# One DVE operation for the block scales of two tensors, residual additions and a context snapshot at other places of the step: an attention and FP4 FFN block on one core

## Chip, cores and metric

One core of a Trainium2 chip runs the whole program. The metric is the device time of one execution in microseconds (us), a median over runs. Five engines work side by side, each on its own instruction stream, and meet through semaphores: PE (TensorE, matmuls), DVE (VectorE), ACT (ScalarE), POOL (GpSimd) and SP (SyncE, which issues nearly all DMAs).

## What is computed

x has 8 sequences of 2048 tokens with 256 features. Cut to what matters:

```
xn = layernorm(x)
# causal linear attention over buckets of 64 tokens, 16 heads of 16
q, k, v = split(xn @ W_qkv.T);  q = softmax(q, -1) / 4;  k = exp(k)
context, k_sum = exclusive running sums over buckets of k^T v and of k
attn = (q @ context) / max(q . k_sum, 1e-6)
# FFN, every operand of a product quantized in blocks of 16 to FP4 (E2M1)
scale = max(|block|) / 6, at least 1e-12;  v -> grid(v / scale) * scale
h = silu(Q(xn) @ Q(w_gate).T) * (Q(xn) @ Q(w_up).T)
out = x + attn @ W_out.T + Q(h) @ Q(w_down).T
```

## The kernel before, in words

The 16384 tokens are cut into 128 tiles of 128 tokens (the same bucket of 64 tokens of two sequences), and the weights are quantized once at the start. There is no scheduler: each engine has a hand-written function `step(n, d)` that handles tile k = 2n + d, and each engine runs all its steps in that written order. `par` is d, `odd` is 1 - d, and most buffers are double by that parity. The first and last steps are written out, the rest are hardware loops of two steps.

One step works on several tiles at once. In step k:

- **PE** does `project_qkv(k+1)` (q, k, v into two PSUM banks of `unit`), `bucket(k)` (the numerators into `nump`, then the sums into `ctxp`), `gate_up(k, 0)` and `gate_up(k, 1)` (the two halves of the FFN's 704 columns), `transpose_q(k+1)` (L1101, two fp32 transposes into `trp`), `project_att(k-2)` (L1074 to L1078 into `outp`) and `project_h(k-2)` (L1165 to L1168 into `outp`). `project_att(k-2)` waits until DVE has added up tile k-3, since both use `outp`.
- **ACT** does `high_att`, `exp_k`, `exp_q(k+1)` (L556, waits for `shift_q`), the wide copies of the scales (`scales_x` L587, `scales_h` L602), the tanh of both halves (L580), `factor_of_row` (L596), `normalise(k+3)` (L526), `mean_of(k+4)` (L498), `high_xn(k+3)` (L535), `copy_qt(k+1)` (L564, after PE's transposes), `squares_of(k+4)` (L510) and last `snapshot(k+1)` (L617, eight activations that copy the context out of PSUM once PE's `bucket(k)` is done).
- **POOL** does `low_att(k-1)` (L411: att minus its high fp16 part, after ACT's `high_att`), `low_xn(k+3)` (L418, the same for xn after `high_xn`) and `rstd_of(k+4)` (L426 to L436, four operations on one column, after `squares_of`).
- **SP** issues the transposing DMAs `turn_xq(k+1)`, `turn_att(k-1)`, `turn_h(k-1)`, `turn_xn(k+3)` in that order, and every second step a load and a store.
- **DVE** has the longest list: `scale_x(k+1)` (L933, L935), `block_max_x(k+2)` (L834), `block_max_h(k-1)` (L827), `block_scales` (L843 for x, L847 for h), `max_q(k+1)` (L764), `over_one` (L854 row maximum of h's scales, L859 reciprocal of all 60 scales), `row_scale` (L866), `shift_q(k+1)` (L773), `over_row` (L873), the two divisions `over_scales_h` (L880) and `over_scales_x` (L887), the two roundings `round_hx` (L901, L909), between them and behind them the two parts of `add_up(k-3)` (L958, L963), then gate, up, attention and `scale_h(k-1)` (both parts L922).

`block_scales` before is two instructions on neighbouring parts of one tile `blk` (44 columns of h, 16 of x), each multiplying by a constant and taking the maximum with a floor: a constant for x, a value in SBUF (`h_floor`) for h:

```
nc.vector.tensor_scalar(xblk[:, 1, :], xblk[:, 0, :], SIX_TIE * 2.0 ** 11, XS * TINY * 2.0 ** 11, ALU.mult, ALU.max)
nc.vector.tensor_scalar(hblk[:, 1, :], hblk[:, 0, :], SIX_TIE * 2.0 ** 11, h_floor[:, :], ALU.mult, ALU.max)
```

Of the kernel before, what the change touches and what calls it, by code (L numbers as in the profile page):

```python
# [5 lines left out]
def linear_attention_fp4_ffn_block(nc, x, wqkv_t, wout_t, wgate, wup, wdown, out):  # L6
# [59 lines left out]
    with ctx:  # L66
# [75 lines left out]
        hblk, xblk = blk[:, :, 0:FB], blk[:, :, FB:FB + XB]  # L142
        xs_hi = sb("xs_hi", [P, 2 * XB], bf16)
# [65 lines left out]

        hx_step = sem("hx_step")  # L210
# [50 lines left out]
        def _(sp):  # L261
# [31 lines left out]
            def turn_xq(t, par):  # L293
                if not is_tile(t):
                    return
                sp.wait_ge(xq_step, after(t, 6))
                sp.sem_inc(sp_turn, 1)
                if begun(t - 2):
                    sp.wait_ge(gu_done, after(t - 2, 2))
                sp.sem_inc(sp_turn, 1)  # L300
                sp.dma_start_transpose(xqt[:, par, :, :].rearrange("p s (c k) -> p (s c) k", k=P),
                                       xq_s[:, par, :, :].rearrange("p s k -> p (s k)")).then_inc(xqt_done[par], 16)

            def turn_h(t, par):
                if not is_tile(t):
                    return
                sp.wait_ge(hq_step, after(t, 9))
# [156 lines left out]
        def _(act):  # L464
# [49 lines left out]
            def normalise_waits(t):  # L514
                if not is_tile(t):
                    return
                act.wait_ge(rstd_step, after(t, 4))
                if begun(t - 2):
                    act.wait_ge(xn_lo, after(t - 2))
                if begun(t - 2):  # L520
                    act.wait_ge(xq_step, after(t - 2, 6, 3))
# [61 lines left out]
            def scales_x(t):  # L583
                if not is_tile(t):
                    return
                act.wait_ge(xq_step, after(t, 6, 2))
                nc.scalar.activation(xs_hi[:, :].rearrange("p (b i) -> p b i", i=2), twice(xblk[:, 1, :]), ACT.Copy)\  # L587
                    .then_inc(x_scaled, 1)

            def factor_of_row(t, par):  # L590
                if not is_tile(t):
                    return
                act.wait_ge(hq_step, after(t, 9, 4))
# [4 lines left out]
            def scales_h(t):  # L598
                if not is_tile(t):
                    return  # L600
                act.wait_ge(hq_step, after(t, 9, 5))
# [18 lines left out]
            def step(n, d):  # L620
# [6 lines left out]
                tanh_gate(k, 0, par)  # L627
                normalise_waits(k + 3)
# [45 lines left out]
        def _(dve):  # L674
# [139 lines left out]
            def times_up(t, half, par):  # L814
# [3 lines left out]
                if begun(t - 2):  # L818
                    dve.wait_ge(hq_step, after(t - 2, 9, 6))
# [20 lines left out]
            def block_scales(t, u):  # L840
                if is_tile(u):
                    dve.wait_ge(xq_step, after(u, 6, 1))
                    nc.vector.tensor_scalar(xblk[:, 1, :], xblk[:, 0, :], SIX_TIE * 2.0 ** 11, XS * TINY * 2.0 ** 11, ALU.mult, ALU.max)\  # L843
                        .then_inc(xq_step, 1)
                if is_tile(t):
                    dve.wait_ge(hq_step, after(t, 9, 1))
                    nc.vector.tensor_scalar(hblk[:, 1, :], hblk[:, 0, :], SIX_TIE * 2.0 ** 11, h_floor[:, :], ALU.mult, ALU.max)\  # L847
                        .then_inc(hq_step, 1)

            def over_one(t, u):  # L850
                do_h, do_x = is_tile(t), is_tile(u)
# [39 lines left out]
            def round_hx(t, u, part):  # L891
# [4 lines left out]
                if part == 0:  # L896
                    if do_h:
                        dve.wait_ge(hq_step, after(t, 9, 6))
                    if do_x:
                        dve.wait_ge(xq_step, after(u, 6, 3))  # L900
                    nc.vector.tensor_scalar(hx_u[:, both], hx_v[:, both].bitcast(bf16)[:, 1:2 * (both.stop - both.start):2],  # L901
                                            SHRINK, None, ALU.mult).then_inc(hx_step, 1)
                if part == 1:
                    dve.wait_ge(hx_step, hx_after(u, 2))
                    if begun(t - 1):
                        dve.wait_ge(hq_step, after(t - 1, 9))
                    if begun(u - 1):
                        dve.wait_ge(xq_step, after(u - 1, 6))
# [3 lines left out]
            def scale_h(t, par, part):  # L912
# [7 lines left out]
                else:  # L920
                    dve.wait_ge(hq_step, after(t, 9, 7))
# [3 lines left out]
            def scale_x(t, par):  # L925
# [4 lines left out]
                dve.wait_ge(xq_step, after(t, 6, 4))  # L930
# [35 lines left out]
            def step(n, d):  # L966
# [71 lines left out]
            nc.vector.tensor_scalar(h_floor[:, :], h_floor[:, :], 2.0 * TINY * 2.0 ** 11, None, ALU.mult).then_inc(factors, 1)  # L1038
            step(-2, 0)
# [12 lines left out]
            dve.wait_ge(factors, 11)  # L1052
# [12 lines left out]
        def _(pe):  # L1065
# [105 lines left out]
            def step(n, d, ends=False):  # L1171
# [97 lines left out]
```

## Time and profile before

| what | value |
|---|---|
| median of 3 runs | 1360.32 us (1359.64 to 1360.74) |
| the profiled execution | 1361.72 us, its span 1360.0 us |
| busy share of the span: DVE, PE, ACT, POOL | 96%, 93%, 71%, 26% |
| mean granted TensorE clock over the span | 0.989 of full speed |
| HBM read and written | 19.99 MB and 16.78 MB, 27 GB/s over the span |

A row of a timeline begins with an instruction's start and its duration in us. On DVE and ACT the next instruction may start before the one ahead has ended, so the cost of an instruction in a full stream is the distance from its start to the next start, not its duration. "Idle" behind a row is the time its engine had nothing running before it, and who ended that.

### The profile page before, as it was taken

To read this page: it belongs to the slowest core of one execution; us is meant where nothing else is said; L and a number is where in the kernel's file an instruction comes from. 1 tells how busy PE (TensorE), PEld (TensorE's weight loads), DVE (VectorE), ACT (ScalarE), POOL (GpSimd) and SP (SyncE) were. 2 spreads that over 40 slices of the span, in tenths; PEclk is the share of its full clock that TensorE was granted. 3 is DMA by queue.
4 is the path that set the end of the run, shared out by engine and by line. 5 is a ranking of instruction groups with operands and counts; after the bars stand their busy time and mean duration, and the time that the engine had idled before them with its cause. 6 is when DMAs were issued, how large, how long until landed. Compare 5 with 4: busy or idle time off the path is not lost.

```text
span 1360.0 us, 41012 instructions
## 1 busy us (share of the span) xinstructions
PE 1271.1 (93%) x9934; PEld 871.0 (64%) x9934; DVE 1309.7 (96%) x3901; ACT 969.4 (71%) x3221; POOL 355.0 (26%) x791
## 2 busy tenths in 40 slices
PE   0279999999999999999999999999999999999996
PEld 0157666666666666666666666666666666666664
DVE  6869999999999999999999999999999999999996
ACT  1567777777777777777777777777777777777772
POOL 2212223222222323222222222223232222323220
PEclk9889999999999999999999999999999999999998
DMA  4024544444454444444544444545454454445444
GB/s 129 12 40 82 108 98 100 105 100 102 98 114 100 101 105 98 103 100 98 113 101 105 98 102 99 112 98 104 105 109 99 92 115 101 96 105 110 97 83 91
DMA packets 432380, 133.64 MB, mean 98 GB/s; under 512 B 397404, under 2 KB 431836, under 8 KB 432348
## 3 DMA queue, kind: packets, MB, share of 16 engines
q1 hardware_dynamic: 431622, 132.60, 46.8%
q10 hardware_dynamic: 726, 0.72, 0.2%
q14 instruction: 24, 0.20, 0.0%
q8 instruction: 8, 0.13, 0.0%
HBM read 19.99 MB, written 16.78 MB: 27 GB/s over the span
## 4 chain that ended last, share of the span: by engine, by line
DVE 52%; issue 33%; DVEq 7%; PE 5%; ACT 2%; DMA 1%; SPq 0%; ACTq 0%
DVE hx_v L880 7%; DVE ga L810 5%; DVE blk L834 3%; DVE xring L963 3%; DVE hx_v L887 3%; DVE h L820 2%; DVE drec L794 2%; DVE xq_s L935 2%; DVE q_rows L922 2%; DVE att L799 2%; DVE osum L958 2%; DVE blk L843 1%; DVE dz L786 1%; DVE hrow L854 1%; DVE dmx L790 1%
## 5 line engine op out<-in xcount | busy, mean ns | idle before, releaser
L418 POOL TENSOR_TENSOR xn_s<-xn,xn_s 128x256 f16<-128x256 f32 x128 | 108.6, 848 | 820.3 <-ACT xn_s L535 820.3
L1165 PE MATMUL outp<-w_down_cat,q_rows 128*128 128x256 f16 x1408 | 246.1, 274 | 0.0
L617 ACT ACTIVATE snap<-ctxp,mask 64x68 f32<-64x68 f32 x1024 | 236.5, 310 | 3.3
L1165 PEld LDWEIGHTS outp<-w_down_cat,q_rows 128*128 128x128 f16 x1408 | 138.3, 98 | 16.5
L1167 PE MATMUL outp<-w_down_lo,q_rows 128*128 128x256 f16 x640 | 147.6, 274 | 0.0
L580 ACT ACTIVATE th<-unit0a,c_g 128x352 f32<-128x352 f32 x128 | 71.0, 554 | 97.3 <-PE unit0b L1078 95.3
L556 ACT ACTIVATE qexp<-qsh,c_q 128x256 f32<-128x256 f32 x128 | 65.1, 508 | 99.0 <-DVE qsh L773 98.8
L580 ACT ACTIVATE th<-unit1a,c_g 128x352 f32<-128x352 f32 x128 | 71.0, 555 | 87.4 <-PE unit1b L1078 65.0
L827 DVE TENSOR_REDUCE blk<-h 128x44 f32<-128x704 f32 x128 | 123.8, 967 | 0.1
L411 POOL TENSOR_TENSOR att_s<-att,att_s 128x256 f16<-128x256 f32 x128 | 87.9, 687 | 108.1 <-ACT att_s L572 108.1
L880 DVE TENSOR_TENSOR hx_v<-h,blk 128x704 f32<-128x704 f32 x128 | 111.0, 868 | 0.0
L1115 PE MATMUL nump<-snap,qt 128*64 128x144 f32 x1024 | 91.2, 299 | 4.7 <-ACT snap L617 4.6
L901 DVE TENSOR_SCALAR hx_u<-hx_v 128x960 f16<-128x960 bf16 (+2 forms) x131 | 85.0, 649 | 4.9
L1074 PE MATMUL outp<-w_out,att_t 128*128 128x256 f16 x256 | 71.2, 278 | 17.7 <-DVE xring L963 15.6
L1115 PEld LDWEIGHTS nump<-snap,qt 128*64 128x64 f32 x1024 | 56.7, 136 | 45.3 <-issue 39.3
L1074 PE MATMUL unit1a<-w_gate,xqt 128*128 128x352 f16 x256 | 80.9, 316 | 0.4 <-DMA xqt<-xq_s 0.4
L1074 PE MATMUL unit0a<-w_gate,xqt 128*128 128x352 f16 x256 | 80.7, 315 | 0.0
L432 POOL TENSOR_TENSOR rstd<-var_eps,neg_half 128x1 f32<-128x1 f32 x128 | 77.8, 608 | 10.0
L1076 PE MATMUL unit1b<-w_up,xqt 128*128 128x352 f16 x256 | 80.2, 313 | 0.0
L1076 PE MATMUL unit1a<-w_gate,xqt 128*128 128x352 f16 x256 | 80.2, 313 | 0.0
L1074 PE MATMUL unit1b<-w_up,xqt 128*128 128x352 f16 x256 | 80.2, 313 | 0.0
L1078 PE MATMUL unit1b<-w_up,xqt 128*128 128x352 f16 x256 | 80.2, 313 | 0.0
(199 smaller groups left out, 4059.0 us busy)
## 6 DMA issues: line engine op xcount, KB each, us to landing
xring<-x SPq DMA_DIRECT2D x128, 128.0 KB, 2.7
out<-xring SPq DMA_DIRECT2D x128, 128.0 KB, 2.5
xnt<-xn_s SPq DMA_TRANSPOSE x128, 2.5
xqt<-xq_s SPq DMA_TRANSPOSE x128, 2.4
att_t<-att_s SPq DMA_TRANSPOSE x128, 2.5
q_rows<-q_rows SPq DMA_TRANSPOSE x128, 3.6
raw_qkv<-wqkv_t SPq DMA_DIRECT2D x1, 768.0 KB, 4.4
raw_up<-wup ACTq DMA_DIRECT2D x2, 352.0 KB
```

The costliest lines, as they stand in the source:

```text
L411: nc.gpsimd.tensor_tensor(att_s[:, par, 1, :], att[:, par, :], att_s[:, par, 0, :], ALU.subtract)\
L418: nc.gpsimd.tensor_tensor(xn_s[:, par, 1, :], xn[:, par, :], xn_s[:, par, 0, :], ALU.subtract).then_inc(xn_lo, 1)
L580: nc.scalar.activation(th[:, half, :], unit[(par + half) % 2][0][:, 0:FH], ACT.Tanh, scale=c_g[:, :])\
L617: nc.scalar.activation(kept[:, :, cols], sums[:, :, cols], ACT.Copy, scale=mask[rows, f, h:h + 1])\
L827: nc.vector.tensor_reduce(hblk[:, 0, :], h[:, par, :].rearrange("p (o b i) -> p b o i", b=FB, i=2), AX.XY, ALU.max, apply_absolute_value=T ...
L880: nc.vector.tensor_tensor(rows(hx_v[:, 0:F]), rows(h[:, par, :]), pairs_of(hblk[:, 2, :]), ALU.mult)\
L901: nc.vector.tensor_scalar(hx_u[:, both], hx_v[:, both].bitcast(bf16)[:, 1:2 * (both.stop - both.start):2], SHRINK, None, ALU.mult).then_in ...
L1074: nc.tensor.matmul(o, stat_hi, m, start=first, stop=False)
L1076: nc.tensor.matmul(o, stat_hi, m, start=False, stop=False)
L1115: last = nc.tensor.matmul(nump[rows, g * 2 * SW:(g + 1) * 2 * SW], qt[:, par, g * P + s * BUCKET:g * P + (s + 1) * BUCKET], snap[:, g, s, ...
L1165: nc.tensor.matmul(downp, hqt[:, par, m, :], w_down_cat[:, m, :], start=(m == 0), stop=False)
L1167: nc.tensor.matmul(downp, hqt[:, par, m, :], w_down_lo[:, m, :], start=False, stop=False)
```

## The change

Five edits, all in what each engine does within a step:

1. `block_scales` becomes one `scalar_tensor_tensor` over all 60 columns; the floors stand in a new tile `blk_floor` [128, 60], filled once at the start by a memset and a copy. It has its own semaphore `blk_scaled`, so that the counts of `xq_step` and `hq_step` per tile fall from 6 and 9 to 5 and 8.
2. On DVE `max_q` comes ahead of `block_scales`.
3. On DVE `add_up` part 0 comes ahead of `over_one`, and part 1 ahead of `over_scales_h`.
4. On ACT `snapshot` comes between the two tanhs, `squares_wait` ahead of `high_xn`, and `copy_qt` last.
5. On PE `transpose_q` comes last, behind `project_h`.

```
             def scales_x(t):
-                act.wait_ge(xq_step, after(t, 6, 2))
+                act.wait_ge(blk_scaled, t + 1)
...
             def block_scales(t, u):
-                if is_tile(u):
-                    dve.wait_ge(xq_step, after(u, 6, 1))
-                    nc.vector.tensor_scalar(xblk[:, 1, :], xblk[:, 0, :], SIX_TIE * 2.0 ** 11, XS * TINY * 2.0 ** 11, ALU.mult, ALU.max)\
-                        .then_inc(xq_step, 1)
-                if is_tile(t):
-                    dve.wait_ge(hq_step, after(t, 9, 1))
-                    nc.vector.tensor_scalar(hblk[:, 1, :], hblk[:, 0, :], SIX_TIE * 2.0 ** 11, h_floor[:, :], ALU.mult, ALU.max)\
-                        .then_inc(hq_step, 1)
+                do_h, do_x = is_tile(t), is_tile(u)
+                if do_h:
+                    dve.wait_ge(hq_step, after(t, 8, 1))
+                if do_x:
+                    dve.wait_ge(xq_step, after(u, 5, 1))
+                if do_h or do_x:
+                    both = slice(0 if do_h else FB, FB + XB if do_x else FB)
+                    nc.vector.scalar_tensor_tensor(blk[:, 1, both], blk[:, 0, both], SIX_TIE * 2.0 ** 11, blk_floor[:, both],
+                                                   ALU.mult, ALU.max).then_inc(blk_scaled, 1)
...
             def over_one(t, u):
                 if do_h:
-                    dve.wait_ge(hq_step, after(t, 9, 2))
+                    dve.wait_ge(blk_scaled, t + 4)
...
 # ACT's step
                 tanh_gate(k, 0, par)
+                snapshot(k + 1)
                 normalise_waits(k + 3)
                 mean_waits(n, d + 4)
                 tanh_gate(k, 1, par)
                 factor_of_row(k - 1, odd)
                 normalise(n, d + 3)
                 mean_of(n, d + 4)
+                squares_wait(k + 4)
                 high_xn(k + 3, odd)
-                squares_wait(k + 4)
+                squares_of(n, d + 4)
                 copy_qt(k + 1, odd)
-                squares_of(n, d + 4)
-                snapshot(k + 1)
...
 # DVE's step
                 block_max_h(k - 1, odd)
+                max_q(k + 1, odd)
                 block_scales(k - 1, k + 2)
-                max_q(k + 1, odd)
+                add_up(n, d - 3, 0)
                 over_one(k - 1, k + 2)
                 row_scale(k - 1)
                 shift_q(k + 1, odd)
                 over_row(k - 1)
+                add_up(n, d - 3, 1)
                 over_scales_h(k - 1, odd)
                 over_scales_x(k + 2, par)
                 round_hx(k - 1, k + 2, 0)
-                add_up(n, d - 3, 0)
                 round_hx(k - 1, k + 2, 1)
-                add_up(n, d - 3, 1)
...
 # once, ahead of DVE's steps
+            nc.vector.memset(blk_floor[:, FB:FB + XB], XS * TINY * 2.0 ** 11).then_inc(factors, 1)
+            dve.wait_ge(factors, 12)
+            nc.vector.tensor_copy(blk_floor[:, 0:FB], h_floor[:, :].broadcast_to([P, FB])).then_inc(factors, 1)
...
 # PE's step
                 gate_up(k, 1, par)
-                transpose_q(k + 1, odd)
                 project_att(k - 2, par)
                 project_h(k - 2, par)
+                transpose_q(k + 1, odd)
```

How the rows of a step move, at three places. On DVE, from the maximum of h's blocks to the division of h (`blk` holds block maxima, scales and their reciprocals, `osum` is part 0 of `add_up`, `xring` part 1); before:

```order
L827 TENSOR_REDUCE blk<-h 128x44
L843 TENSOR_SCALAR blk<-blk 128x16
L847 TENSOR_SCALAR blk<-blk,h_floor 128x44
L764 TENSOR_REDUCE qmax<-unit0b 128x16
L854 TENSOR_REDUCE hrow<-blk 128x1
L859 RECIPROCAL blk<-blk 128x60
L866 TENSOR_SCALAR hrow<-hrow 128x1
L773 TENSOR_TENSOR qsh<-unit0b,qmax 128x256
L873 RECIPROCAL hrow<-hrow 128x1
L880 TENSOR_TENSOR hx_v<-h,blk 128x704
```

and with the change (a line of before is here two to three higher):

```order
L829 TENSOR_REDUCE blk<-h 128x44
L766 TENSOR_REDUCE qmax<-unit0b 128x16
L850 SCALAR_TENSOR_TENSOR blk<-blk,blk_floor 128x60
L961 SCALAR_TENSOR_TENSOR osum<-outp,c_o,xring 128x256
L857 TENSOR_REDUCE hrow<-blk 128x1
L862 RECIPROCAL blk<-blk 128x60
L869 TENSOR_SCALAR hrow<-hrow 128x1
L775 TENSOR_TENSOR qsh<-unit0b,qmax 128x256
L876 RECIPROCAL hrow<-hrow 128x1
L966 SCALAR_TENSOR_TENSOR xring<-outp,c_row,osum 128x256
L883 TENSOR_TENSOR hx_v<-h,blk 128x704
```

Two instructions became one, the q maximum now stands between the h maximum and the scales, and both additions stand ahead of the division.

On DVE, the two roundings (`hx_u`, `hx_q`) a little later in the same step, before:

```order
L887 TENSOR_TENSOR hx_v<-xn,blk 128x256
L901 TENSOR_SCALAR hx_u<-hx_v 128x960
L958 SCALAR_TENSOR_TENSOR osum<-outp,c_o,xring 128x256
L909 TENSOR_SCALAR hx_q<-hx_u 128x960
L963 SCALAR_TENSOR_TENSOR xring<-outp,c_row,osum 128x256
L810 SCALAR_TENSOR_TENSOR ga<-th,unit1a 128x352
```

and with the change:

```order
L890 TENSOR_TENSOR hx_v<-xn,blk 128x256
L904 TENSOR_SCALAR hx_u<-hx_v 128x960
L912 TENSOR_SCALAR hx_q<-hx_u 128x960
L812 SCALAR_TENSOR_TENSOR ga<-th,unit1a 128x352
L944 TENSOR_TENSOR xs_lo<-blk,xs_hi 128x32
```

The second rounding, which reads what the first writes, now follows it directly.

On ACT, from the first tanh (`th`) to the next step's `att_s`, before:

```order
L580 ACTIVATE th<-unit0a,c_g 128x352
L580 ACTIVATE th<-unit1a,c_g 128x352
L596 ACTIVATE c_row<-hrow,c_d 128x1
L526 ACTIVATE xn<-xring,shift,rstd 128x256
L498 ACTIVATE scratch,neg_mean<-xring 128x256
L535 ACTIVATE xn_s<-xn 128x256
L564 ACTIVATE qt<-trp 128x256
L510 ACTIVATE scratch,squares<-xring,neg_mean 128x256
L617 ACTIVATE snap<-ctxp,mask 64x4x17 x8
L572 ACTIVATE att_s<-att 128x256
```

and with the change:

```order
L582 ACTIVATE th<-unit0a,c_g 128x352
L619 ACTIVATE snap<-ctxp,mask 64x4x17 x8
L582 ACTIVATE th<-unit1a,c_g 128x352
L598 ACTIVATE c_row<-hrow,c_d 128x1
L528 ACTIVATE xn<-xring,shift,rstd 128x256
L500 ACTIVATE scratch,neg_mean<-xring 128x256
L537 ACTIVATE xn_s<-xn 128x256
L512 ACTIVATE scratch,squares<-xring,neg_mean 128x256
L566 ACTIVATE qt<-trp 128x256
L574 ACTIVATE att_s<-att 128x256
```

The eight activations of the snapshot moved from the end of the step to between the tanhs, and the copy of the transposed q is now the last of the step.

## Rows read from the trace of the kernel before

**Rows 1.** Windows: busy PE, PEld, DVE, ACT, POOL, then clock, DMA, GB/s.

```profile
750.00:1250.00 500.00, 495.49 (x3887) 339.04 (x3886) 497.38 (x1518) 374.90 (x1267) 137.81 (x306) 1.00 0.49 103
```

**Rows 2.** Source view of L786, 250 to 1250 us: min/median/max ns, starts.

```profile
L786 DVE COPY dz<-nump x101: 164/168/171, 252.8 to 1243.7; 128x16 f32<-128x16 f32 x101
```

**Rows 3.** Groups on DVE, 250 to 1250 us: busy us, mean ns.

```profile
L847 DVE TENSOR_SCALAR blk<-blk,h_floor 128x44 f32<-128x44 f32 x101 | 37.0, 366 | 0.0
L945 DVE SCALAR_TENSOR_TENSOR hs_lo<-blk,hrow,hs_hi 128x88 f16<-128x88 f32 x101 | 30.7, 304 | 0.0
...
L843 DVE TENSOR_SCALAR blk<-blk 128x16 f32<-128x16 f32 x101 | 26.6, 263 | 0.0
```

**Rows 4.** Source view of L843, same stretch: duration ns min/median/max.

```profile
L843 DVE TENSOR_SCALAR blk<-blk x101: 158/234/643, 256.9 to 1247.8; 128x16 f32<-128x16 f32 x101
```

**Rows 5.** Timeline of DVE, from scale_x to q's maximum.

```profile
413.50 0.29 DVE L933 TENSOR_TENSOR xq_s<-hx_q,xs_hi 128x256 f16<-128x256 f16 x1
...
414.24 0.97 DVE L827 TENSOR_REDUCE blk<-h 128x44 f32<-128x704 f32 x1
415.13 0.55 DVE L843 TENSOR_SCALAR blk<-blk 128x16 f32<-128x16 f32 x1
415.59 0.23 DVE L847 TENSOR_SCALAR blk<-blk,h_floor 128x44 f32<-128x44 f32 x1
415.75 0.41 DVE L764 TENSOR_REDUCE qmax<-unit1b 128x16 f32<-128x256 f32 x1
```

**Rows 6.** Timeline of POOL, the same step.

```profile
412.00 0.69 POOL L418 TENSOR_TENSOR xn_s<-xn,xn_s 128x256 f16<-128x256 f32 x1 [6.45 <-ACT xn_s L535]
412.76 0.19 POOL L426 TENSOR_TENSOR var_scaled<-squares,var_mul 128x1 f32<-128x1 f32 x1
...
413.93 0.19 POOL L436 TENSOR_TENSOR shift<-neg_mean,rstd 128x1 f32<-128x1 f32 x1
414.98 0.67 POOL L411 TENSOR_TENSOR att_s<-att,att_s 128x256 f16<-128x256 f32 x1 [0.86 <-ACT att_s L572]
```

**Rows 7.** Timeline of DVE, the roundings a little later.

```profile
418.27 0.66 DVE L901 TENSOR_SCALAR hx_u<-hx_v 128x960 f16<-128x960 bf16 x1
418.85 0.48 DVE L958 SCALAR_TENSOR_TENSOR osum<-outp,c_o,xring 128x256 f32<-128x256 f32 x1
419.24 0.40 DVE L909 TENSOR_SCALAR hx_q<-hx_u 128x960 uint16<-128x960 uint16 x1
```

**Rows 8.** Waits between 250 and 1250 us: total us, times, longest.

```profile
PEld outp L1074 <- DVE xring L963: 25.6, 68, 0.8
```

**Rows 9.** Timeline of PE: a whole step, from one project_qkv to the next.

```profile
403.04 0.39 PE L1074 MATMUL unit0a<-w_qkv,xnt 128*128 128x512 f16 x1
...
409.79 0.38 PE L1101 MATMUL trp<-ident,qexp 128*128 128x128 f32 x2
410.01 0.28 PE L1074 MATMUL outp<-w_out,att_t 128*128 128x256 f16 x1
...
412.73 0.39 PE L1074 MATMUL unit1a<-w_qkv,xnt 128*128 128x512 f16 x1
```

**Rows 10.** Timeline of ACT, the same step.

```profile
406.98 0.51 ACT L556 ACTIVATE qexp<-qsh,c_q 128x256 f32<-128x256 f32 x1 [0.64 <-DVE qsh L773]
...
408.20 0.55 ACT L580 ACTIVATE th<-unit1a,c_g 128x352 f32<-128x352 f32 x1 [0.34 <-PE unit1b L1078]
410.00 0.55 ACT L580 ACTIVATE th<-unit0a,c_g 128x352 f32<-128x352 f32 x1 [1.24 <-PE unit0b L1078]
...
411.52 0.40 ACT L535 ACTIVATE xn_s<-xn 128x256 f16<-128x256 f32 x1
...
412.58 1.87 ACT L617 ACTIVATE snap<-ctxp,mask 64x68 f32<-64x68 f32 x8
```

**Rows 11.** Timeline of POOL at the start of the program.

```profile
96.42 0.67 POOL L418 TENSOR_TENSOR xn_s<-xn,xn_s 128x256 f16<-128x256 f32 x1 [7.55 <-ACT xn_s L535]
```

**Rows 12.** Timeline of DVE beside it.

```profile
96.58 0.66 DVE L933 TENSOR_TENSOR xq_s<-hx_q,xs_hi 128x256 f16<-128x256 f16 x1
```

More of the change, by code:

```diff
@@ L142, in linear_attention_fp4_ffn_block @@
         hblk, xblk = blk[:, :, 0:FB], blk[:, :, FB:FB + XB]
+        blk_floor = sb("blk_floor", [P, FB + XB])
         xs_hi = sb("xs_hi", [P, 2 * XB], bf16)
@@ L295, in turn_xq @@
                     return
-                sp.wait_ge(xq_step, after(t, 6))
+                sp.wait_ge(xq_step, after(t, 5))
                 sp.sem_inc(sp_turn, 1)
@@ L306, in turn_h @@
                     return
-                sp.wait_ge(hq_step, after(t, 9))
+                sp.wait_ge(hq_step, after(t, 8))
                 sp.sem_inc(sp_turn, 1)
@@ L520, in normalise_waits @@
                 if begun(t - 2):
-                    act.wait_ge(xq_step, after(t - 2, 6, 3))
+                    act.wait_ge(xq_step, after(t - 2, 5, 2))
             def normalise(n, d):
@@ L592, in factor_of_row @@
                     return
-                act.wait_ge(hq_step, after(t, 9, 4))
+                act.wait_ge(hq_step, after(t, 8, 3))
                 if begun(t - 2):
@@ L600, in scales_h @@
                     return
-                act.wait_ge(hq_step, after(t, 9, 5))
+                act.wait_ge(hq_step, after(t, 8, 4))
                 nc.scalar.activation(hs_hi[:, :].rearrange("p (b i) -> p b i", i=2), twice(hblk[:, 1, :]), ACT.Copy,
@@ L818, in times_up @@
                 if begun(t - 2):
-                    dve.wait_ge(hq_step, after(t - 2, 9, 6))
+                    dve.wait_ge(hq_step, after(t - 2, 8, 5))
                 nc.vector.tensor_tensor(h[:, par, half * FH:(half + 1) * FH], ga[:, half, :],
@@ L856, in over_one @@
                     if do_x:
-                        dve.wait_ge(xq_step, after(u, 6, 2))
+                        dve.wait_ge(blk_scaled, u + 1)
                     both = slice(0 if do_h else FB, FB + XB if do_x else FB)
@@ L862, in row_scale @@
                 if is_tile(t):
-                    dve.wait_ge(hq_step, after(t, 9, 3))
+                    dve.wait_ge(hq_step, after(t, 8, 2))
                     if begun(t - 1):
@@ L871, in over_row @@
                     return
-                dve.wait_ge(hq_step, after(t, 9, 4))
+                dve.wait_ge(hq_step, after(t, 8, 3))
                 nc.vector.reciprocal(hrow[:, 2, :], hrow[:, 1, :]).then_inc(hq_step, 1)
@@ L897, in round_hx @@
                     if do_h:
-                        dve.wait_ge(hq_step, after(t, 9, 6))
+                        dve.wait_ge(hq_step, after(t, 8, 5))
                     if do_x:
-                        dve.wait_ge(xq_step, after(u, 6, 3))
+                        dve.wait_ge(xq_step, after(u, 5, 2))
                     nc.vector.tensor_scalar(hx_u[:, both], hx_v[:, both].bitcast(bf16)[:, 1:2 * (both.stop - both.start):2],
@@ L905, in round_hx @@
                     if begun(t - 1):
-                        dve.wait_ge(hq_step, after(t - 1, 9))
+                        dve.wait_ge(hq_step, after(t - 1, 8))
                     if begun(u - 1):
-                        dve.wait_ge(xq_step, after(u - 1, 6))
+                        dve.wait_ge(xq_step, after(u - 1, 5))
                     nc.vector.tensor_scalar(hx_q[:, both], hx_u[:, both].bitcast(u16), GRID16, -GRID16, ALU.add, ALU.add)\
@@ L920, in scale_h @@
                 else:
-                    dve.wait_ge(hq_step, after(t, 9, 7))
+                    dve.wait_ge(hq_step, after(t, 8, 6))
                 nc.vector.tensor_tensor(rows(hq_s[:, par, part * F:(part + 1) * F]), rows(hx_q[:, 0:F].bitcast(fp16)),
@@ L929, in scale_x @@
                 dve.wait_ge(hx_step, hx_after(t, 3))
-                dve.wait_ge(xq_step, after(t, 6, 4))
+                dve.wait_ge(xq_step, after(t, 5, 3))
                 if begun(t - 2):
```

3 lines of the change are left out of this document (2 added, 1 removed).

## The prediction

> **What bounds the kernel now.** I read the windows first, then the waits, then timelines of one step. The windows say that two engines are full: from 750 to 1250 us DVE is busy 497.4 us of 500 and PE 495.5, at a granted clock of 1.00; ACT is at 75% and POOL at 28% [rows 1]. The two full engines are told apart by who waits. No DVE instruction in the stretch waits for another engine long enough to be listed, and its groups show an idle time of 0.0 [rows 3]. PE does wait, 68 times in 101 steps, ahead of the att projection, for `add_up` part 1 [rows 8]. So DVE sets the pace. `L786` runs once a step, 101 times from 252.8 to 1243.7 us [rows 2], so a step takes 990.9 / 100 = 9.91 us, and 128 steps are nearly the whole span.
>
> PE is close behind. Between two `project_qkv` without a wait there lie 412.73 - 403.04 = 9.69 us; this step's transposes begin at 409.79 and the att projection follows 0.22 later [rows 9]. The waits in the waits view, 25.6 / 101 = 0.25 us a step [rows 8], contain the end of the transposes' weight loads, so they agree with 9.91 - 9.69 = 0.22. **If DVE became free, the most that a step can lose is 0.22 us.**
>
> DVE's 9.91 us are not all work. `L843` is 0.158 us alone but 0.263 in the mean and up to 0.643 [rows 3, 4], and `L847` is 0.23 alone [rows 5] but 0.366 in the mean [rows 3]. Together that is 0.105 + 0.136 = 0.24 us a step. One step shows where it comes from: POOL's `L411` runs from 414.98 to 415.65 [rows 6], and `L843`, which starts at 415.13, ends at 415.68 rather than 415.29 [rows 5]. `L827`, running at the same time, has its usual length. Without these stalls DVE needs 9.91 - 0.24 = 9.67 us.
>
> **The change, part by part.**
>
> *Joined scales.* Uncontended the pair costs from start to start 0.16 for `L847` [rows 5] and at least 0.158 less the overlap of 0.08 that every row has with the next (`L827` is 0.97 long, the next starts 0.89 later, rows below it), so 0.08: some 0.24, and a little more for the order of their waits. The price of one operation over 60 columns is in no row. Below stands the 16 column one with 0.158, above the 88 column one of the same kind, `L945`, with 0.304 [rows 3, 4]. Less 0.08 these are 0.08 and 0.22; by width, 0.17. I take 0.16, and the join is worth **-0.08** (bounds -0.16 and -0.02).
>
> *Second rounding behind the first.* Before, `L958` filled the time in which `L901` finishes: `L909` starts at 419.24. Now it follows directly, but reads what `L901` writes, so it cannot start when `L958` did (418.85) but only after the end at 418.93 and a wake-up. The nearest row for that is on POOL, where `L426` starts 0.07 behind the end of `L418` [rows 6]; I take 0.04 as an estimate between nothing and that. The hole is **+0.12** and nothing covers it (bounds +0.08 and +0.15) [rows 7].
>
> *`max_q` ahead of the scales, `add_up` ahead of reciprocal and division.* The same instructions at other places: 0 of work. `max_q` covers the end of `L827` as `L843` did; `add_up` 0 covers the end of the scales as `max_q` did. What is queued behind is `shift_q`, now later by the 0.40 of `add_up` 0 [rows 7] less the join. For it wait `exp_q`, which began at 406.98, and `gate_up(k, 1)`, whose first matmul began as the first tanh's input was ready, at 408.20 [rows 10]: over 0.8 us of cover is left. `max_q` itself needs `qkv_done`, and stands 0.3 earlier; if PE is the slower engine DVE waits here, which costs nothing.
>
> *`add_up` some 1.5 to 2.5 us earlier.* This frees `outp` before PE has ended `gate_up(k, 1)`. The wait of rows 8 goes: **PE falls from 9.91 to 9.69**. What it would wait for next is far: h of the tile before for `gate_up(k, 0)`.
>
> *Transposes last on PE.* Same two fp32 operations, again between fp16 neighbours. No row shows them behind the last down projection; I take 0, bounds -0.1 (their 0.22 [rows 9] half hidden) and +0.14 (the start of the loads not hidden). `copy_qt` comes later, but `bucket(k+1)` needs it only 2 us into the next step, behind `project_qkv`.
>
> *Snapshot between the tanhs.* ACT had idle time ahead of the second tanh, 1.24 us in this step [rows 10], and the snapshot takes 1.87. So the second tanh starts near 408.65 + 1.87 = 410.5 instead of 410.0, and `gate_h(k, 1)` on DVE, the reader, comes over 1.5 us behind that. `high_xn` then starts at 411.52 + 0.45 + 0.1 (its new wait) = 412.1, and POOL's `L418` near 412.6 instead of 412.00, ending at 413.3. `att_s` no longer waits behind the snapshot, which ended at 414.45. It is ready by 413.6. But POOL has its four one-column operations first: they last 414.12 - 412.76 = 1.36 [rows 6], now from 413.3 to 414.6, so `L411` runs from 414.7 to 415.4. No step of these issues a DMA; SP's order is unchanged, its four turning DMAs have tiles of lead.
>
> *Do the stalls go?* The joined operation would start 0.89 + 0.33 after `L827`'s 414.24, at about 415.4: just when `L411` ends. I book the 0.24 as gone, and keep 0.02 for edges. One rule speaks against this change. In the Trainium skill, "SBUF — State Buffer", "Who interferes with whom", an operation of DVE with two inputs in SBUF is blocked by a GpSimd operation that reads SBUF, whatever its mode. By that rule the join does not take the operation out of POOL's reach, since `blk_floor` is a second input; only its new place can. The trace has a case that agrees: `L933`, with two inputs in SBUF, takes 0.66 instead of 0.29 [rows 5, 12] while POOL's `L418` runs to 97.09 [rows 11]. That page's rule is the first rival.
>
> *Once.* A memset and a copy with their waits ahead of the first step: at most +0.5, I take +0.4. The last additions at the end of the program are behind PE as before: 0.
>
> **The sum.** DVE: 9.67 - 0.08 + 0.12 = 9.71. PE: 9.69. They are now level, with little between them, and I take 9.72 for a step. That is 0.19 less than 9.91, over some 126 steps at this pace -24 us, +0.4 once. Against the profiled execution, 1361.7 us, that is 1338.1; it lay 1.4 above the median of the runs, so the forecast for the median is **1337 us**.
>
> **The rivals.**
>
> *A. The joined operation keeps half the stall.* If `L411` stays at 414.98 to 415.65, the operation at 415.4 is held for 0.25 in such steps and none in the others, 0.13 in the mean, and DVE takes 9.84: 126 x 0.07 = 9 us less, **1352**. For it: the page's rule and the held `L933` [rows 11, 12]. Against: both ends of POOL's work move earlier, as worked out. Chance 0.13.
>
> *B. The transposes cost PE more at their new place.* PE at 9.69 + 0.12 = 9.81: 126 x 0.10 = 13 less, **1348**. For: they change data type behind the one matmul with 64 rows. Against: their old place also lay between fp16 neighbours. Chance 0.1.
>
> *C. The other side: POOL's `L418` meets `scale_x`.* It ended at 412.69, 0.8 before `L933` at 413.50 [rows 5, 6]; I place its end at 413.3. Were ACT 0.2 us later than I think, `L933` would be held as at the start of the program [rows 11, 12], at most the 0.67 of `L418`. It decides at a hold of 0.20 in the mean, since 9.71 + 0.20 = 9.91. At 0.45, DVE takes 10.16: 126 x 0.25 = 31 more, **1392**. Against: a later DVE gives `L418` more room, since ACT follows PE at the tanh, so the hold shrinks as it appears. Chance 0.07.
>
> *D. The change gives nothing*: the hole at the rounding eats the join and the stall only moves to `row_scale` or the roundings, which are single-input operations of the same kind as `L843`. They start over 1 us after `L411`'s end. **1359**, chance 0.04.
>
> *E. More than forecast*: the PE floor itself is lower by 0.1 through the transposes, and the hole is small: 1327. Chance 0.06.
>
> **How the numbers follow.** The forecast (1331 to 1343, steps of 9.67 to 9.77) has 0.60. The range should leave out at most 0.2: from 1329 to 1353 it holds the forecast, B and most of A, and leaves C, D and part of E. A measurement of this kernel tells 0.2% (2.7 us) from nothing. Faster: forecast, A, B, E, 0.89; same: D with the upper edge of A, 0.04; slower: C, 0.07.
>
> **What would show it.** In the new profile: `L961`, `L966` ahead of the division, the joined `L850` near 0.22 to 0.25 with a maximum not over 0.4 (A: up to 0.6 in half the steps); `L912` starting 0.70 behind `L904` instead of 0.58 for the next instruction; no wait of the att projection on `add_up`; PE busy over 99% and DVE waiting for `qkv_done` at `max_q` in short pieces; `L936` and `L938` at 0.29 (C: one of them over 0.4); a step of 9.70 to 9.74. The forecast is wrong if DVE is still never idle and its step is above 9.8, and the term to look at then is whichever of these rows grew.

## The result, and the profile after

| | before | changed |
|---|---|---|
| median | 1360.53 us | 1370.36 us (1368.74 to 1370.90, 4 runs) |
| ratio, 95% interval | 1 | 1.0071, 1.0054 to 1.0089 |
| span of the profiled execution | 1360.0 us | 1368.6 us |
| one step, from 250 to 1250 us | 9.91 us | 10.00 us |

The change makes the kernel 0.7% slower; 1337 us, 1.7% faster, was forecast. The windows of the changed kernel, in the columns of [rows 1]:

```profile
750.00:1250.00 500.00, 494.46 (x3846) 334.32 (x3844) 483.43 (x1451) 372.08 (x1253) 124.73 (x300) 1.00 0.48 102
```

Neither of the two engines gained: PE has 494.5 busy instead of 495.5, DVE 483.4 instead of 497.4. DVE now has 3.3% of idle time, which the forecast allowed only as waits for PE. The step, in the source view of the line that was `L786` [rows 2]: (1242.5 - 252.6) / 99 = 10.00 us.

```profile
L788 DVE COPY dz<-nump x100: 166/168/171, 252.6 to 1242.5; 128x16 f32<-128x16 f32 x100
```

The waits of the same stretch, as in [rows 8]:

```profile
PEld unit1a L1080 <- issue: 36.8, 96, 0.9
...
DVE hx_q L912 <- DVE hx_u L904: 22.4, 100, 0.2
...
PE unit1a L1080 <- DVE qsh L775: 10.0, 49, 0.2
```

The wait of the att projection on the addition is gone, as forecast. In its place DVE waits for itself, 22.4 us in 100 steps, ahead of the second rounding, and PE now waits for `shift_q` at the second half of `gate_up`. The groups of DVE, as in [rows 3]:

```profile
L904 DVE TENSOR_SCALAR hx_u<-hx_v 128x960 f16<-128x960 bf16 x100 | 65.9, 659 | 3.4
...
L912 DVE TENSOR_SCALAR hx_q<-hx_u 128x960 uint16<-128x960 uint16 x100 | 41.0, 410 | 22.4 <-DVE hx_u L904 22.4
L850 DVE SCALAR_TENSOR_TENSOR blk<-blk,blk_floor 128x60 f32<-128x60 f32 x100 | 20.9, 209 | 0.0
```

The joined scales, `L850`, take 0.209 us in the mean and never more than 0.230 in this stretch: POOL holds them in no step. The same place in the timeline, as in [rows 5]:

```profile
415.80 0.97 DVE L829 TENSOR_REDUCE blk<-h 128x44 f32<-128x704 f32 x1
416.69 0.41 DVE L766 TENSOR_REDUCE qmax<-unit1b 128x16 f32<-128x256 f32 x1
417.02 0.21 DVE L850 SCALAR_TENSOR_TENSOR blk<-blk,blk_floor 128x60 f32<-128x60 f32 x1
417.32 0.48 DVE L961 SCALAR_TENSOR_TENSOR osum<-outp,c_o,xring 128x256 f32<-128x256 f32 x1
```

and POOL beside it, as in [rows 6]:

```profile
414.11 0.67 POOL L420 TENSOR_TENSOR xn_s<-xn,xn_s 128x256 f16<-128x256 f32 x1 [7.22 <-ACT xn_s L537]
414.74 0.20 POOL L428 TENSOR_TENSOR var_scaled<-squares,var_mul 128x1 f32<-128x1 f32 x1
...
416.03 0.19 POOL L438 TENSOR_TENSOR shift<-neg_mean,rstd 128x1 f32<-128x1 f32 x1
416.35 0.67 POOL L413 TENSOR_TENSOR att_s<-att,att_s 128x256 f16<-128x256 f32 x1
```

`L413` ends at 417.02, in the moment in which `L850` starts. So the whole stall of before went. What came in its place is the distance from `L904` to `L912`, as in [rows 7]:

```profile
410.21 0.66 DVE L904 TENSOR_SCALAR hx_u<-hx_v 128x960 f16<-128x960 bf16 x1
411.09 0.41 DVE L912 TENSOR_SCALAR hx_q<-hx_u 128x960 uint16<-128x960 uint16 x1 [0.22 <-DVE hx_u L904]
411.42 0.51 DVE L812 SCALAR_TENSOR_TENSOR ga<-th,unit1a 128x352 f32<-128x352 f32 x1
```

0.88 us, where the forecast had 0.70. **The sum by gaps**, start to start in the mean of the loops: `L843` and `L847` cost 0.48 together before, `L850` costs 0.26, the hole at the rounding is 0.884 - 0.576 = 0.31, and the rest is within 0.03: -0.48 + 0.26 + 0.31 = +0.09, which is 10.00 - 9.91.

### The profile page after: what moved, and what is told of

Read it like the earlier page. It is cut to its first block, busy times and chain, and to the rows that moved or that the text cites. A ratio compares the mean times of both kernels' runs of the same rounds, so it can differ in the third digit from the quotient of the medians.

```text
span 1368.6 us, 40774 instructions
## 1 busy us (share of the span) xinstructions
PE 1279.0 (93%) x9934; PEld 865.9 (63%) x9934; DVE 1286.3 (94%) x3778; ACT 972.5 (71%) x3221; POOL 329.8 (24%) x791
## 4 chain that ended last, share of the span: by engine, by line
DVE 60%; issue 27%; DVEq 6%; PE 0%; DMA 0%; ACT 0%; SPq 0%
DVE blk L829 8%; DVE hx_v L883 8%; DVE hx_u L904 6%; DVE ga L812 5%; DVE hx_v L890 3%; DVE h L822 3%; DVE blk L836 2%; DVE drec L796 2%; DVE xq_s L936 2%; DVE q_rows L925 2%; DVE hrow L857 2%; DVE att L801 2%; DVE xq_s L938 2%; DVE dz L788 2%; DVE dmx L792 1%
## 5 line engine op out<-in xcount | busy, mean ns | idle before, releaser
L420 POOL TENSOR_TENSOR xn_s<-xn,xn_s 128x256 f16<-128x256 f32 x128 | 87.1, 680 | 938.3 <-ACT xn_s L537 938.3
L829 DVE TENSOR_REDUCE blk<-h 128x44 f32<-128x704 f32 x128 | 124.4, 972 | 0.1
L413 POOL TENSOR_TENSOR att_s<-att,att_s 128x256 f16<-128x256 f32 x128 | 86.3, 674 | 32.6 <-ACT att_s L574 24.7
L904 DVE TENSOR_SCALAR hx_u<-hx_v 128x960 f16<-128x960 bf16 (+2 forms) x131 | 84.9, 648 | 4.8
L1080 PE MATMUL unit0a<-w_gate,xqt 128*128 128x352 f16 x256 | 81.1, 317 | 1.2 <-DVE qsh L775 1.1
L1084 PE MATMUL unit0b<-w_up,xqt 128*128 128x352 f16 x256 | 80.0, 313 | 0.0
L1082 PE MATMUL unit0b<-w_up,xqt 128*128 128x352 f16 x256 | 80.0, 313 | 0.0
L1084 PE MATMUL unit0a<-w_gate,xqt 128*128 128x352 f16 x256 | 80.0, 312 | 0.0
```

Source lines behind the costliest of these rows:

```text
L413: nc.gpsimd.tensor_tensor(att_s[:, par, 1, :], att[:, par, :], att_s[:, par, 0, :], ALU.subtract)\
L420: nc.gpsimd.tensor_tensor(xn_s[:, par, 1, :], xn[:, par, :], xn_s[:, par, 0, :], ALU.subtract).then_inc(xn_lo, 1)
L829: nc.vector.tensor_reduce(hblk[:, 0, :], h[:, par, :].rearrange("p (o b i) -> p b o i", b=FB, i=2), AX.XY, ALU.max, apply_absolute_value=T ...
L1080: nc.tensor.matmul(o, stat_hi, m, start=first, stop=False)
L1082: nc.tensor.matmul(o, stat_hi, m, start=False, stop=False)
L1084: end = nc.tensor.matmul(o, stat_lo, m, start=False, stop=last)
```

## Why the hole is 0.31: two theories

The same kernel has the same pair of instructions, with the same three waits ahead of the second, in the first steps, which are written out and not in a loop, so that the counts waited for are constants:

```profile
110.29 0.66 DVE L904 TENSOR_SCALAR hx_u<-hx_v 128x960 f16<-128x960 bf16 x1
110.99 0.41 DVE L912 TENSOR_SCALAR hx_q<-hx_u 128x960 uint16<-128x960 uint16 x1
```

0.70 there and 0.88 in the loops. The loops' semaphore counts are registers, so between `L904` and `L912` stand operations of DVE's own queue, which the source view lists as DVEq. Of those between the two roundings, the first in the queue and the one just ahead of `L912`:

```profile
L907 DVEq ALU_OP  x1: 40/40/40, 410.2 to 410.2; - x1
```

```profile
L911 DVEq ALU_OP  x1: 40/40/40, 410.9 to 410.9; - x1
```

`L907` is done at 410.2, while the first rounding runs. `L911` runs at 410.9, after its end at 410.87, because it stands behind the wait on the first rounding (`hx_step`). Theory Q (for queue): that is the cost. Theory L (for latency): the result itself comes late when other engines are busy, and the queue is beside the point.

### e1_wait_last

```
 # round_hx, part 1, of the changed kernel
-                    dve.wait_ge(hx_step, hx_after(u, 2))
                     if begun(t - 1):
                         dve.wait_ge(hq_step, after(t - 1, 8))
                     if begun(u - 1):
                         dve.wait_ge(xq_step, after(u - 1, 5))
+                    dve.wait_ge(hx_step, hx_after(u, 2))
```

> The changed kernel; only the order of three waits ahead of the second rounding (L912) differs: the two that are long satisfied come first, the one on the first rounding last. Theory Q (queue): in the hardware loops register operations stand behind the wait on the first rounding, and DVE's queue works them off only after it; they make 0.18 of the 0.88 us from L904 to L912, which is 0.70 in the steps written out. Expects 0.70 in the loops too, a step of 9.82 instead of 10.00 us, 1348 us. Theory L (latency): the first rounding's result is only there 0.22 us after its end while other engines are busy. Expects 0.88 and 1370 us as before.

Measured: 1348.03 us, ratio 0.991 [0.9894, 0.9927]. The rounding in the loop:

```profile
404.58 0.66 DVE L904 TENSOR_SCALAR hx_u<-hx_v 128x960 f16<-128x960 bf16 x1
405.28 0.41 DVE L912 TENSOR_SCALAR hx_q<-hx_u 128x960 uint16<-128x960 uint16 x1
```

```profile
L911 DVEq ALU_OP  x1: 40/40/40, 404.7 to 404.7; - x1
```

0.70, and the queue's `L911` now runs at 404.7, under the first rounding. Theory L falls. Three waits in another order are worth 22 us of this kernel, and a step takes 9.80.

### e13_wait_middle

```
+                    if begun(t - 1):
+                        dve.wait_ge(hq_step, after(t - 1, 8))
                     dve.wait_ge(hx_step, hx_after(u, 2))
-                    if begun(t - 1):
-                        dve.wait_ge(hq_step, after(t - 1, 8))
                     if begun(u - 1):
                         dve.wait_ge(xq_step, after(u - 1, 5))
```

> e1_wait_last with the wait on the first rounding in the middle of the three instead of last: the same three waits and the same number of queue operations in all, but now L912 itself stands behind the blocking operation and carries another, long satisfied wait. Theory Q in its exact form (what counts is whether the instruction itself does the waiting): one place is enough to lose, 0.88 from L904 to L912 in both kinds of step, 10.0 a step, 1370 us. If the loss were in the number of operations left behind the wait (two in half of the changed kernel's steps, one here), 0.79, 1359 us. If it were the number of operations in all, 0.70 as in e1, 1348 us.

Measured: 1358.51 us, ratio 0.9976 [0.9967, 0.9986].

```profile
406.04 0.66 DVE L904 TENSOR_SCALAR hx_u<-hx_v 128x960 f16<-128x960 bf16 x1
406.82 0.41 DVE L912 TENSOR_SCALAR hx_q<-hx_u 128x960 uint16<-128x960 uint16 x1
```

0.78 in every step of the loops: neither end, but the case of one wait left behind the one on the first rounding. The strict form of theory Q, in which one such place costs all of it (0.88), is refuted. With 0.70 for none left behind and 0.88 for the two of the changed kernel, that is some 0.09 us for each wait with a register value that the queue has to work off after the one that blocks. The rows of the queue do not add up to it. In the changed kernel `L909`, the first of the two waits left behind, is one operation in half of the steps and another in the rest:

```profile
L909 DVEq EVENT_SEMAPHORE  x50: 21/21/21, 250.4 to 1230.1; - x50
L909 DVEq FUSED_REGOPS  x50: 53/53/53, 261.0 to 1240.8; - x50
```

The distance is 0.88 in the one kind of step and 0.89 in the other, and the 40 ns of `L911` are less than half of 0.09. So the number of waits left behind fits all three kernels, but what inside such a wait takes the time is not shown.

### e10_fewer_waits

A like loss shows behind `L850`, which itself waits for a result of DVE: the addition `L961` comes some 0.30 us later in one kind of step (417.02 to 417.32 above) and 0.22 in the other, but 0.13 in the steps written out at the end:

```profile
1316.66 0.21 DVE L850 SCALAR_TENSOR_TENSOR blk<-blk,blk_floor 128x60 f32<-128x60 f32 x1
1316.79 0.48 DVE L961 SCALAR_TENSOR_TENSOR osum<-outp,c_o,xring 128x256 f32<-128x256 f32 x1
```

```
 # on top of e1_wait_last: add_up, part 0
-                    if begun(t - 2):
-                        dve.wait_ge(o_step, after(t - 2, 2))
```

> e1_wait_last without the wait on o_step ahead of part 0 of the addition (DVE itself made that value two steps before). In the loops three queue operations stand between L850 and the addition in one step and two in the other, and the addition comes 0.30 and 0.21 behind L850, 0.13 in the steps written out. Theory Q: one operation fewer is worth 0.09 each, so 0.21 and 0.13, a step of 9.80 - 0.09 = 9.71, and then PE's 9.73 with the transposes last is the bound: 9.73 to 9.77, 1340 us. If the distance is the scales' own latency, 0.26 in the mean stays and 1348 us with it.

Measured: 1337.16 us, ratio 0.983 [0.9814, 0.9846]; from `L850` to the addition 0.18 in the mean instead of 0.26, and a step of 9.72. One wait fewer gave 0.08, near the 0.09 expected, although `L850` itself is held again here in 5 of 103 steps, up to 0.43.

```profile
408.51 0.22 DVE L850 SCALAR_TENSOR_TENSOR blk<-blk,blk_floor 128x60 f32<-128x60 f32 x1
408.71 0.48 DVE L959 SCALAR_TENSOR_TENSOR osum<-outp,c_o,xring 128x256 f32<-128x256 f32 x1
```

```profile
750.00:1250.00 500.00, 500.00 (x3956) 348.47 (x3954) 495.33 (x1494) 382.01 (x1290) 126.25 (x306) 1.00 0.50 105
```

PE is busy all the time and waits for `shift_q` no more. This is the fastest kernel of the study, level with e11 below, with every edit of the change in it. Its time is the one forecast for the change, reached only with the cost of these waits taken out.

### e11_fewer_waits_turn_early

```
 # on top of e10: PE's step
                 gate_up(k, 1, par)
+                transpose_q(k + 1, odd)
                 project_att(k - 2, par)
                 project_h(k - 2, par)
-                transpose_q(k + 1, odd)
```

> e10 with PE's transposes at their old place. PE's floor is 9.69 there against 9.73. If PE sets e10's pace, this gives 0.03 to 0.04 a step, 1336 us; if DVE sets it, the same as e10 within 2 us.

Measured: 1337.38 us, ratio 0.9832 [0.9816, 0.9849]: the same as e10, with the same step of 9.72. PE needs 0.03 less with its transposes early (9.69, from the trace of before) and gains nothing, so DVE's own sum is 9.72 too.

### e2_low_between

```
                 round_hx(k - 1, k + 2, 0)
+                low_scales(k - 1, k + 2)
                 round_hx(k - 1, k + 2, 1)
                 gate_h(k, 0, par)
-                low_scales(k - 1, k + 2)
                 times_up(k, 0, par)
```

> The changed kernel with low_scales (L944, L948, 0.32 us together) between the two roundings instead of behind gate_h. Both theories of the gap expect it filled: L904 to L912 0.90 with the two inside, a step of 10.00 - 0.30 = 9.70, which is also what PE needs; 1332 us. If instead each wait costs its own queue time behind whatever stands ahead (a stronger form of Q), L912 comes at 1.05 and the step is 9.87, 1353 us.

Measured: 1352.20 us, ratio 0.9937 [0.9921, 0.9954]. The time is that of the second expectation, the reason is neither:

```profile
407.30 0.66 DVE L904 TENSOR_SCALAR hx_u<-hx_v 128x960 f16<-128x960 bf16 x1
407.87 0.18 DVE L944 TENSOR_TENSOR xs_lo<-blk,xs_hi 128x32 f16<-128x32 f32 x1
407.97 0.30 DVE L948 SCALAR_TENSOR_TENSOR hs_lo<-blk,hrow,hs_hi 128x88 f16<-128x88 f32 x1
408.19 0.40 DVE L912 TENSOR_SCALAR hx_q<-hx_u 128x960 uint16<-128x960 uint16 x1
408.51 0.51 DVE L812 SCALAR_TENSOR_TENSOR ga<-th,unit1a 128x352 f32<-128x352 f32 x1
409.06 0.52 DVE L822 TENSOR_TENSOR h<-ga,unit1b 128x352 f32<-128x352 f32 x1
```

The hole is filled, `L904` to `L912` is 0.89. But `low_scales` had been the cover of another pair: `times_up` (`L822`) multiplies what `gate_h` (`L812`) makes. With nothing between them it starts 0.55 later in one kind of step and 0.64 in the other, where `L944` had started 0.43 after `L812`. A filler taken from between two dependent instructions opens the hole it came from.

## The parts of the change alone

### e5_adds_only

```
 # the kernel before, DVE's step
                 max_q(k + 1, odd)
+                add_up(n, d - 3, 0)
                 over_one(k - 1, k + 2)
                 row_scale(k - 1)
                 shift_q(k + 1, odd)
                 over_row(k - 1)
+                add_up(n, d - 3, 1)
                 over_scales_h(k - 1, odd)
                 over_scales_x(k + 2, par)
                 round_hx(k - 1, k + 2, 0)
-                add_up(n, d - 3, 0)
                 round_hx(k - 1, k + 2, 1)
-                add_up(n, d - 3, 1)
```

> The kernel before with edit 3 alone (both additions early). If the hole between the roundings is this edit's and its size does not depend on the others: L901 to L909 0.88 instead of 0.97 with an addition of 0.40 between, so a hole of 0.31; PE no longer waits for L963; the stalls at L843 and L847 keep their 0.24. A step of 9.91 + 0.31 = 10.2 us, 1397 us. If instead an earlier addition gives PE and so DVE something, a step under 10.1.

Measured: 1419.83 us, ratio 1.0424 [1.0407, 1.0442], a step of 10.38, slower than either expectation. The hole is as in the changed kernel (0.88). `L843` and `L847` are free of POOL here, 0.28 together to the next start. But POOL's other large operation, `L418`, now meets `scale_h`. One step, DVE and then POOL:

```profile
416.58 0.52 DVE L922 TENSOR_TENSOR q_rows<-hx_q,hs_hi 128x704 f16<-128x704 f16 x1
...
417.09 0.92 DVE L922 TENSOR_TENSOR q_rows<-hx_q,hs_lo 128x704 f16<-128x704 f16 x1
```

```profile
416.70 0.93 POOL L418 TENSOR_TENSOR xn_s<-xn,xn_s 128x256 f16<-128x256 f32 x1 [6.78 <-ACT xn_s L535]
```

`L418` starts beside the first half of `scale_h` and is long itself, 0.93 instead of the 0.67 that it takes in the changed kernel; the second half starts while it still runs. All steps, in the source view, min/median/max ns:

```profile
L922 DVE TENSOR_TENSOR q_rows<-hx_q,hs_hi x97: 509/515/519, 250.5 to 1246.8; 128x704 f16<-128x704 f16 x97
L922 DVE TENSOR_TENSOR q_rows<-hx_q,hs_lo x97: 905/910/917, 251.0 to 1247.3; 128x704 f16<-128x704 f16 x97
```

Every one of 97 second halves is held, 0.91 instead of 0.52. By starts: 9.91 - 0.20 + 0.30 + 0.37 = 10.38. The stall did not vanish with the new order, it took another victim, and a dearer one.

### e12_act_only and e3_act_pe_only

```
 # e12: the kernel before with ACT's step of the change
                 tanh_gate(k, 0, par)
+                snapshot(k + 1)
...
 # e3: as e12, and PE's step of the change
                 gate_up(k, 1, par)
-                transpose_q(k + 1, odd)
                 project_att(k - 2, par)
                 project_h(k - 2, par)
+                transpose_q(k + 1, odd)
```

> The kernel before with edit 4 alone (ACT's order). e3 with edits 4 and 5 took 9.97 a step, 0.07 more than before, as its two scale operations were stalled for 0.06 more and L933 for 0.03. If that is ACT's order alone, 9.97 and 1369 us again; if the late transposes are part of it, which lie on the way from PE's last wait to qkv_done, 9.91 and 1361 us.

> The kernel before with edits 4 and 5 alone (snapshot between the tanhs, squares_wait, copy_qt last, transposes last); DVE as before. Theory P (place): the stalls of 0.24 us a step at L843 and L847 come from where POOL's L411 lies, and moving ACT's work moves it away: L843 at 0.17 and L847 at 0.23 in the mean, a step of 9.67 to 9.72, 1333 us. Theory O (operation): only the join takes them away; L843 and L847 keep means of 0.26 and 0.37, a step near 9.9, 1360 us.

Measured: e12 1361.63 us, ratio 1.0004 [0.9994, 1.0014]; e3 1368.79 us, ratio 1.0063 [1.0046, 1.0080]. Groups of e12, then of e3, to be read against [rows 3]:

```profile
L843 DVE TENSOR_SCALAR blk<-blk 128x16 f32<-128x16 f32 x101 | 44.5, 441 | 0.0
...
L847 DVE TENSOR_SCALAR blk<-blk,h_floor 128x44 f32<-128x44 f32 x101 | 24.0, 237 | 0.0
```

```profile
L843 DVE TENSOR_SCALAR blk<-blk 128x16 f32<-128x16 f32 x100 | 36.6, 366 | 0.0
L847 DVE TENSOR_SCALAR blk<-blk,h_floor 128x44 f32<-128x44 f32 x100 | 33.1, 331 | 0.0
```

ACT's new order moved the stall from `L847` (0.366 to 0.237) to `L843` (0.263 to 0.441) and left the time where it was. With the late transposes both are held: from the start of `L843` to the next start behind `L847` it is 0.54 in the mean, 0.51 in e12 and 0.48 before. Theory P, that the place alone frees the scales, is refuted; the 1360 us of theory O is missed by 9. The 0.07 that a step of e3 (9.98) is longer than before is, by starts, 0.07 at these two and 0.03 at `L933`, less 0.03 at the second `L922`. What shifts POOL against DVE there was not tried by itself and stays open.

### e4_join_only

```
 # the changed kernel with additions, ACT's and PE's steps as before; what is left is
                 block_max_h(k - 1, odd)
+                max_q(k + 1, odd)
                 block_scales(k - 1, k + 2)      # one scalar_tensor_tensor
-                max_q(k + 1, odd)
```

> Edits 1 and 2 alone (joined scales behind max_q); additions, ACT and PE as before. If POOL's reading operations block any DVE operation with two SBUF inputs, the joined one keeps part of the stall in ACT's old order: up to 0.5 long in some steps, a mean of 0.30, a step of 9.75 to 9.85, 1345 us. If it is free of POOL, it is 0.21 in all steps, and a step takes 9.91 - 0.48 + 0.26 = 9.69, 1334 us.

Measured: 1347.12 us, ratio 0.9908 [0.9891, 0.9924], a step of 9.78, as the first expectation has it. DVE of two steps, then POOL of the same:

```profile
480.72 0.46 DVE L850 SCALAR_TENSOR_TENSOR blk<-blk,blk_floor 128x60 f32<-128x60 f32 x1
481.21 0.20 DVE L857 TENSOR_REDUCE hrow<-blk 128x1 f32<-128x44 f32 x1
...
490.67 0.21 DVE L850 SCALAR_TENSOR_TENSOR blk<-blk,blk_floor 128x60 f32<-128x60 f32 x1
490.91 0.20 DVE L857 TENSOR_REDUCE hrow<-blk 128x1 f32<-128x44 f32 x1
```

```profile
480.42 0.68 POOL L413 TENSOR_TENSOR att_s<-att,att_s 128x256 f16<-128x256 f32 x1 [0.69 <-ACT att_s L574]
...
490.05 0.68 POOL L413 TENSOR_TENSOR att_s<-att,att_s 128x256 f16<-128x256 f32 x1 [0.79 <-ACT att_s L574]
```

In one step `L850` starts 0.30 behind the start of POOL's `L413`, whose 0.68 end at 481.10, and is 0.46 long; in the other it starts 0.06 before POOL's end and has its usual 0.21. Its mean is 0.33. So neither the join alone nor the new order on ACT and PE alone (e3, e12) takes the stall away, and both together without the early additions do not either (e6 below); in the changed kernel, with all of them, it is gone. And an operation with two inputs in SBUF is held by a reading POOL operation although it is not a `tensor_scalar`; the page named in the prediction ("SBUF — State Buffer", "Who interferes with whom", of the Trainium skill) says so, and the trace agrees.

### e6_adds_back, e8_join_act and e9_adds_split

```
 # e6: the changed kernel, DVE's step
                 round_hx(k - 1, k + 2, 0)
+                add_up(n, d - 3, 0)
                 round_hx(k - 1, k + 2, 1)
+                add_up(n, d - 3, 1)
 # (and both gone from their early places)
 # e8: as e6, and PE's transposes ahead of project_att
 # e9: as e8, but
                 over_row(k - 1)
+                add_up(n, d - 3, 0)
                 over_scales_h(k - 1, odd)
...
                 round_hx(k - 1, k + 2, 0)
+                add_up(n, d - 3, 1)
                 round_hx(k - 1, k + 2, 1)
```

> The changed kernel without edit 3: the additions behind the two roundings as before, the rest changed. The hole is gone (-0.31) and the scales cost 0.23 to the next start instead of 0.26: DVE at 9.66. PE measures 9.73 with its transposes last, and the wait of its att projection on the addition is back in part. Expects a step of 9.73 to 9.78, 1338 us; if L850 meets POOL's L413 in this order, its mean rises over 0.25 and the step to 9.8.

> As e6, but PE's transposes at their old place: edits 1, 2 and 4. Theory T: the transposes last cost PE 0.04 a step (0.274 to the next matmul instead of 0.22, beside small differences), so PE's floor is 9.69 and a step 9.69 to 9.74, 1334 us. If their place does not matter, as e6 within 2 us.

> Edits 1, 2 and 4 with part 0 of the addition ahead of the division of h and part 1 between the roundings: nothing uncovered on DVE, and outp free 0.3 us earlier than in e8. Expects the wait of the att projection near 0 and both engines at 9.66 to 9.70: 1331 us. If e8 does not wait there either, the same time as e8.

Measured: e6 1353.97 us, ratio 0.9941 [0.9924, 0.9959]; e8 1342.03 us, 0.9857 [0.9841, 0.9874]; e9 1343.02 us, 0.9868 [0.9852, 0.9885]. The changed kernel is 16 us slower than e6, which has the additions where they fill the hole, but e6 is 16 us above its own expectation of 1338. The wait of the att projection on the addition, e6 first, then e8:

```profile
PEld outp L1080 <- DVE xring L966: 32.5, 101, 0.6
```

```profile
PEld outp L1080 <- DVE xring L966: 10.9, 50, 0.4
```

Between e6 and e8 only PE's transposes moved, and that is 12 us, more than twice the 0.04 x 126 = 5 us of PE's own work. In e6 a step takes 9.85, and its rows read as a loop through both engines: the addition releases the att projection, the transposes stand behind it and ahead of `project_qkv`, and `max_q` on DVE waits for that (from `L829` to `L766` 0.95 in the mean, 0.88 in e8). That is 0.07 of the 0.10 between the two steps (e8: 9.75, where 9.69 to 9.74 was expected); most of the rest is `L850`, held a little longer. At their old place PE does the transposes while it would wait for the addition anyway. With the addition early (e10, e11) nothing waits there, and their place makes no difference. e9 has part 1 of the addition 0.3 earlier and is no faster than e8; the wait of the att projection on it did not shrink (13.3 us in 53 steps). Its `L850` is held less (0.211 in the mean, 0.281 in e8), but part 0 of the addition stands behind the one-column `over_row` and comes 0.16 after it, where the division came 0.07 after it. That looks like the queue again and was not tried by itself.

## Why the prediction was wrong

- **What bounds the kernel, and by how much**: right. DVE, with PE 0.22 behind. With the transposes last PE's floor is 9.72, the step of e10, in which PE is never idle: the next matmul follows the transposes by 0.27 instead of 0.22. 0 was taken, +0.14 was the bound.
- **Do the stalls go** (0.24): right in that they went. The size was read from durations; by starts the pair cost 0.48 before and 0.27 to 0.28 free (e5), so 0.20 to 0.21. The forecast put `L411`'s end where the joined operation starts, and so it is. That was in part luck: with the additions back (e6) `L850` is held, to 0.40, in nearly every second step.
- **Second rounding behind the first**, +0.12 with bounds of 0.08 and 0.15: this is the step that failed. It is +0.31. The data part is 0.12, as e1 shows; 0.19 is the queue, which here comes to the two waits behind the blocking one only after it (0.70, 0.78 and 0.88 for none, one and two). My estimate took the wake-up from a POOL row and looked at the engine's rows alone.
- **Joined scales**, -0.08 with bounds of -0.16 and -0.02: failed by less. The pair cost 0.27 without stalls, the joined one costs 0.26, so 0.00. The operation alone costs 0.13 (written-out steps), less than the 0.16 taken; the other 0.13 is the queue ahead of the addition (a wait fewer there gave 0.08 in e10), which my edit-by-edit list put at "0 of work".
- **`add_up` early frees PE**: right, and worth nothing. PE ran ahead and was held at `gate_up(k, 1)` for `shift_q`, where I had counted 0.8 us of cover from the old phase: half to half takes 2.07 instead of 1.80.
- **The sum**: by starts, 9.91 - 0.21 - 0.01 + 0.31 = 10.00. With only two terms corrected, the hole to +0.31 and the join to 0.00, the forecast would have been 9.67 + 0.31 = 9.98 a step, which is slower.
- **The rivals**: C, the only one slower, did not happen; `L936` and `L938` keep 0.29 and 0.28. A's mechanism is real (e4) but did not act in the changed kernel. B's is real at 0.03 to 0.05 a step and did not bind. D had the hole at the rounding eating the join; that much happened, but the hole is twice the largest size forecast. None of them was the queue. The sign named for a wrong forecast, DVE never idle at a step above 9.8, came only half: the step is 10.00, but DVE is idle for 3.3%, mostly in the hole.

## What to carry to other kernels

Where an instruction waits for the one just ahead of it, let that wait be its last, and let no register-valued wait stand behind it: all of them have to be met in any order, and the order was worth 22 us here. Before work is taken from between two dependent instructions, or put there, look at what it covered: here two roundings, and gate and up. The stall between DVE and POOL was a matter of where the two engines' operations lay against each other: each new order moved it or took it away, and only the profile of the new kernel told which.

## What was not expected of the hardware

- A wait with a register value that DVE's queue can only come to after a blocking one costs some 0.09 us on the path, though it is met long before (0.70, 0.78, 0.88 us between the roundings for none, one and two), more than twice the 40 ns shown for its register operation. Ahead of the blocking wait (e1), or with a constant count (the written-out steps), it costs nothing here: 0.70.
- In e5 a `tensor_tensor` of fp16 data takes 0.91 instead of 0.52 beside POOL's `L418` in all 97 steps, and `L418` itself takes 0.93 in the median instead of 0.67. In the changed kernel neither is held in any step (0.52 and 0.67), and the joined scales are held in about every second step of e6. So a stall can strike in every step, in every second one or in none.
